# A prepared seam, table products by halves, twelve gathers, masks placed by ScalarE and an own order for the last routing chunk

## The reference, cut to what matters

```python
x = x + 0.5 * ffn(layernorm(x))
x = x + attention(layernorm(x))
x = x + 0.5 * ffn(layernorm(x))
```

```python
def ffn(xf):                                   # xf: 8192 x 256
    scores = softmax(xf @ gate_w.T)            # 64 experts
    _, idx = top_k(scores + gate_b, 6)
    # every expert takes its first 128 (token, choice) pairs, in the order of tokens
    h  = silu(xb @ w1[e].T) * (xb @ w3[e].T)   # 128 x 176, for each expert
    y[tok] += (h @ w2[e].T) * scores[tok, e]
    z  = silu(xf @ ws1.T) * (xf @ ws3.T) @ ws2.T   # shared expert, all tokens
    return y + z
```

## Time and profile before

| | |
|---|---|
| runs | 1922.69, 1925.52, 1930.68 us (median 1925.52) |
| profiled execution, its own time | 1931.83 us |
| its span | 1929.7 us |
| TensorE busy | 1792.8 us (93%) |
| VectorE, ScalarE, GpSimd busy | 1340.3, 1090.6, 837.2 us |
| mean granted TensorE clock | 0.973 |

### The profile page before, as it was taken

How to read it: one execution, slowest core, us unless ns; L and a number is a source line. 1 busy time by engine, 2 the same in 40 slices (tenths; PEclk the granted TensorE clock), 3 DMA queues, 4 the chain that set the end, 5 groups by cost and what they waited for, 6 DMA issues and landing times. The chain is left out here.

```text
span 1929.7 us, 31890 instructions
## 1 busy us (share of the span) xinstructions
PE 1792.8 (93%) x10553; PEld 1098.0 (57%) x10554; DVE 1340.3 (69%) x3338; ACT 1090.6 (57%) x2260; POOL 837.2 (43%) x923
## 2 busy tenths in 40 slices
PE   5999999999957889999999999999799999989998
PEld 3565665777643345555555555555356666667776
DVE  4887878566547567777777777767278787766665
ACT  4767766111113667777777777777467676731111
POOL 1010100678664666656556665550001010037777
PEclk9999999999988899999999999999899999999999
DMA  2423331899853333333333333332222343339997
GB/s 76 125 84 117 117 109 70 228 261 259 231 126 88 88 84 105 104 102 108 108 98 109 105 100 101 89 89 57 66 72 84 110 124 103 98 109 263 267 262 158
DMA packets 192653, 244.05 MB, mean 126 GB/s; under 512 B 17578, under 2 KB 159978, under 8 KB 192494
## 3 DMA queue, kind: packets, MB, share of 16 engines
q1 hardware_dynamic: 166654, 202.97, 35.0%
q0 software_dynamic: 24576, 37.77, 10.2%
q10 hardware_dynamic: 1264, 1.31, 0.2%
HBM read 126.63 MB, written 63.86 MB: 99 GB/s over the span
## 5 line engine op out<-in xcount | busy, mean ns | idle before, releaser
L1359 DVE TENSOR_REDUCE a_smax<-a_p_ring 128x1 f32<-128x512 f32 (+2 forms) x768 | 355.2, 506 | 131.8 <-PE a_p_ring L1446 126.4
L1263 ACT ACTIVATE a_probs<-a_p_ring 128x512 f32<-128x512 f32 x640 | 368.1, 608 | 108.6 <-PE a_p_ring L1458 107.3
L48 POOL TENSOR_TENSOR f_rstd<-f_mv,eps 128x4 f32<-128x4 f32 x32 | 26.9, 840 | 543.0 <-DVE f_mv L42 538.4
L1446 PE MATMUL a_p_ring<-p_ks,p_qs 100*128 100x512 bf16 (+3 forms) x1024 | 244.7, 304 | 16.7 <-DVE a_smax L1359 5.2
L1458 PE MATMUL a_p_ring<-p_qs,p_ks 103*128 103x512 bf16 (+3 forms) x1024 | 242.9, 304 | 7.9 <-ACT a_probs L1263 6.3
L648 ACT ACTIVATE e_silu<-e_p_up 128x176 f32<-128x176 f32 x128 | 40.6, 317 | 352.8 <-PE e_p_up L738 352.8
L487 PE MATMUL f_p_up<-f_xnT,ws1T 128*128 128x512 f32 x384 | 187.9, 612 | 1.1 <-ACT f_xnT L280 1.1
L528 PE MATMUL f_p_z<-ws2T,f_hidden 128*128 128x256 f32 (+1 forms) x768 | 184.8, 391 | 1.8 <-DVE f_hidden L374 1.8
L127 POOL DMA_INDIRECT h_got<-rows,slot_token x128 | 126.0, 985 | 133.6 <-DVE slot_token L464 86.1
L487 PE MATMUL f_p_up<-f_xnT,ws3T 128*128 128x512 f32 x384 | 181.5, 595 | 0.0
L738 PE MATMUL e_p_up<-h_w,e_xT 128*128 128x352 f32 x512 | 176.8, 469 | 2.6 <-DMA h_w<-w_in 2.6
(11 more groups left out here) (156 smaller groups left out, 3579.1 us busy)
## 6 DMA issues: line engine op xcount, KB each, us to landing
h_w<-w_in SPq DMA_DIRECT2D x128, 352.0 KB
p_qs<-a_parts SPq DMA_DIRECT2D x192, 128.0 KB, 2.4
p_ks<-a_parts SPq DMA_DIRECT2D x192, 128.0 KB, 2.4
h_w<-w_in SPq DMA_DIRECT2D x128, 176.0 KB
rows<-f_row SPq DMA_DIRECT2D x32, 640.0 KB, 6.4
x<-x_in SPq DMA_DIRECT2D x16, 512.0 KB, 5.6
acc<-x SPq DMA_DIRECT2D x16, 512.0 KB, 3.3
a_x<-acc SPq DMA_DIRECT2D x16, 512.0 KB, 3.9
```

The costliest lines, as they stand in the source:

```text
L1263: nc.scalar.activation(to[:], p_score[s][:], ACT.Exp, scale=SCALE).then_inc(score_free[s], 1)
L1359: ins = nc.vector.tensor_reduce(smax[:, t, 4 * g + h:4 * g + h + 1], p_score[s][:, at:at + length], AX.X, ALU.max)
L1446: ins = nc.tensor.matmul(p_score[s][:, at:at + length], qs[1 - u][0:SR + MASK, 4 * g + h, t * P:(t + 1) * P], ks[1 - u][0:SR + MASK, 4 * g ...
```

## The change

1. Halves: add_to_table(c, r) does half of a chunk's 24 products, and TensorE puts one half in front of each turn.
2. Prepared seam: in attention's last turn new steps HEAD_STATS (at 0.72 of the turn: VectorE's statistics and GpSimd's scales of f2's chunk 0, after a wait for its load) and HEAD_NORM 0 to 3 (at 0.83 to 0.92: ScalarE normalises a tile each). f2 skips these for chunk 0.
3. Twelve gathers (GATHERS) ahead instead of eight, with twelve buffers.
4. ScalarE masks: place_masks is gone; ScalarE copies the mask rows in 32 pieces of 7 partitions x 1024 elements, one behind each of experts 24 to 55 of e1.
5. Last chunk: in chunk 14 TensorE does up(15, 2), shared(14, 0), logits(15), shared(14, 1); chunk 15 has an order of its own. ScalarE does write_down(14) behind exponents(15), and silus(15, 1) last; VectorE's add_shared(14, 1) goes behind picked, multiply(15, 1) behind slots. hidden of j = 2 has two buffers.
6. VectorE: pick compares with an operand that is doubled in its innermost place; the ranks' sum is two additions and a shorter sum; the table is finished in three operations instead of four.
7. The semaphore redirected is gone (a drain on VectorE instead), and attention's x are arrivals.x[2:4].

```diff
@@ scalar, route_and_share @@
 def chunk(c, i, u, left):
     exponents(c)
+    if not left:
+        write_down(c - 1)
     silus(c, 0)
     if left:
         normalise(c + 1, *later(i, u, 1))
-    silus(c, 1)
     if left:
+        silus(c, 1)
         evacuate(c + 1, 0)
         evacuate(c + 1, 1)
     cap(c)
-    write_down(c)
+    if left != 1:
+        write_down(c)
     if left:
         logits(c + 1)
         silus(c + 1, 2)
+    else:
+        silus(c, 1)
@@ vector @@
-    if c:
+    if c and left:
         add_shared(c - 1, (c - 1) % XR, 1)
...
-    nc.vector.tensor_copy(topf[:], topi[:, :, 0:K])
+    nc.vector.tensor_copy(topf[:], topi[:, :, 0:K].unsqueeze(3).to_broadcast([P, NT, K, 2]))
...
+    by_twos = [P, NT * K, E // 2, 2]
+    nc.vector.tensor_tensor(pick[:].rearrange("p t k (e n) -> p (t k) e n", n=2),
...
+    if not left:
+        add_shared(c - 1, (c - 1) % XR, 1)
     multiply(c, 0)
-    multiply(c, 1)
+    if left:
+        multiply(c, 1)
...
+    nc.vector.tensor_tensor(half_sum[:], by_pair[:, :, 0:E // 2], by_pair[:, :, E // 2:E], ALU.add)
+    nc.vector.tensor_tensor(half_sum[:, :, 0:E // 4], half_sum[:, :, 0:E // 4],
+                            half_sum[:, :, E // 4:E // 2], ALU.add)
-        nc.vector.tensor_reduce(rank[:], prod[:], AX.X, ALU.add)
+        nc.vector.tensor_reduce(rank[:].rearrange("p t k -> p (t k)"), half_sum[:, :, 0:E // 4],
+                                AX.X, ALU.add)
@@ behind the last chunk @@
     slots(N - 1)
-    add_shared(N - 1, (N - 1) % XR, 0)
+    multiply(N - 1, 1)
     dve.wait_ge(table_added, N)
...
-    add_shared(N - 1, (N - 1) % XR, 1)
+    for r in range(2):
+        add_shared(N - 1, (N - 1) % XR, r)
@@ tensor @@
     up(c, 1)
-    if left:
-        turn(c + 1, 0)
-    if c:
-        add_to_table(c - 1)
-    if left:
-        turn(c + 1, 1)
+    for r in range(2):
+        if c:
+            add_to_table(c - 1, r)
+        turn(c + 1, r)
     ranks(c)
-    shared(c, 0)
-    if left:
+    if left > 1:
+        shared(c, 0)
         up(c + 1, 2)
     else:
-        add_to_table(c)
+        up(c + 1, 2)
+        shared(c, 0)
+        logits(c + 1)
     shared(c, 1)
+def last_chunk(c):
+    up(c, 0)
+    add_to_table(c - 1, 0)
+    add_to_table(c - 1, 1)
+    ranks(c)
+    up(c, 1)
+    add_to_table(c, 0)
+    add_to_table(c, 1)
+    shared(c, 0)
+    shared(c, 1)
@@ experts @@
-                    if pre and e == E - 2 * LANES:
-                        place_masks(sp, w, pre)
+                    if pre and 0 <= e - MASKS_FROM < MASK_PIECES:
+                        place_mask(nc, act, pre, e - MASKS_FROM)
@@ attention @@
+NEXT_STAGE = [(0.72, ("HEAD_STATS",)), (0.83, ("HEAD_NORM", 0)), (0.86, ("HEAD_NORM", 1)), (0.89, ("HEAD_NORM", 2)),
+              (0.92, ("HEAD_NORM", 3))]
-            (B - 1, place(OUTPUTS, TAIL + LATE_MAXIMA)),
+            (B - 1, place(OUTPUTS, TAIL + LATE_MAXIMA + NEXT_STAGE)),
+                        elif kind == "HEAD_NORM":
+                            if step[1] == 0:
+                                act.wait_ge(arrivals.head_scales_ready, 1)
+                            token_normalise(nc, arrivals.x[0], arrivals.head_rstd, arrivals.head_shift,
+                                            arrivals.first_row, [step[1]])
+                        elif kind == "HEAD_STATS":
+                            dve.wait_ge(arrivals.x_loaded[0], 16 * (B // XR) + 16)
```

More of the change, by code:

```diff
@@ L30 @@
 LANES = 8
+GATHERS = 12
 GROUP = 4
@@ L96, in open_handover @@
     to.x_loaded, to.x_rounds = arrivals.x_loaded, layer * B // XR
-    to.gathered, to.gather_rounds = arrivals.gathered, layer * E // LANES
+    to.gathered = arrivals.gathered
+    to.gathers_past = [layer * len(range(s, E, GATHERS)) for s in range(GATHERS)]
     to.weights_loaded, to.first_load = arrivals.weights_loaded, layer * E
@@ L156, in route_and_share @@
         x = to.x
-        row = [sb(f"row{u}", [P, NT, ROW]) for u in range(2)]
+        row = [to.first_row, sb("row1", [P, NT, ROW])]
         stats = sb("stats", [P, NT, 6])
@@ L184, in route_and_share @@
         silu = [sb(f"silu{n}", [P, T]) for n in range(RING)]
-        hidden = [sb(f"hidden{j}", [P, T]) for j in range(3)]
-        table = sb("table", [P, 2, E])
+        hidden = [[sb(f"hidden{j}", [P, T])] for j in range(2)] + [[sb(f"hidden2{n}", [P, T]) for n in range(2)]]
+        table = sb("table", [P, E])
         empty = sb("empty", [P, E])
@@ L272, in _ @@
                 pool.wait_ge(slot_token_ready, 1)
-                for e in range(LANES):
+                for e in range(GATHERS):
                     gather_rows(nc, w, dram, to, e)
@@ L390, in add_shared @@
                                                    ALU.add).then_inc(acc_ready, 1)
-                statistics(0, 0, 0)
+                if head_ready:
+                    dve.sem_inc(stats_ready, 1)
+                else:
+                    statistics(0, 0, 0)
                 set_up()
@@ L992, in load_attention, with place_mask @@
         sp.dma_start(to[:], fro).then_inc(pre.weights_loaded, 16)
[L995 to L1004 removed]
+MASK_HEADS = 2
+MASK_PIECES = 4 * H // MASK_HEADS
+def place_mask(nc, act, pre, piece):
+    if piece == 0:
+        act.wait_ge(pre.mask_ready, 1)
+    rows, heads = slice(SR, SR + MASK + TOP), piece % (H // MASK_HEADS) * MASK_HEADS
+    which = piece // (H // MASK_HEADS)
+    to = (pre.qs[0], pre.ks[0], pre.qs[1], pre.ks[1])[which]
+    ins = nc.scalar.copy(to[rows, heads:heads + MASK_HEADS, :],
+                         pre.mask16[rows, which % 2, :].unsqueeze(1).to_broadcast([MASK + TOP, MASK_HEADS, T]))
+    if piece == MASK_PIECES - 1:
+        ins.then_inc(pre.mask_placed, 1)
 def set_up_attention(nc, dve, w, pre, piece):
@@ L1041, in attention @@
         ident16, qs, ks, v, smax_parts = pre.ident16, pre.qs, pre.ks, pre.v, pre.smax_parts
-        x = [sb(f"x{n}", [P, NT, D]) for n in range(2)]
+        x = arrivals.x[2:4]
         residual = [sb(f"residual{n}", [P, NT, D]) for n in range(2)]
```

117 lines of the change are left out of this document (66 added, 51 removed).

## The result

| | before | after |
|---|---|---|
| median of the runs | 1925.52 us (1922.57 to 1930.68, 7 runs) | 1908.43 us (1902.63 to 1915.96, 7 runs) |
| ratio, 95% interval | | 0.9906, 0.9889 to 0.9923 |
| profiled execution, own time and span | 1931.83, 1929.7 us | 1908.43, 1906.6 us |
| TensorE busy | 1792.8 us (93%) | 1789.8 us (94%) |
| mean granted TensorE clock | 0.973 | 0.976 |

The forecast was 1913.0, range 1902 to 1922. The profiled execution of after is its median one, that of before stood 6.3 above its own. So the spans differ by 23.1 us, and the medians by 17.1.

What follows compares the result with a forecast made beforehand. TensorE, busy for 93% of the span, was taken as the bound. Terms summing to -12.4 took the profiled 1931.8 us to 1919.4, which stands 6.3 above the median, so 1913 us, range 1902 to 1922.

Steps and rivals of the forecast that it cites:

- the clock in the tails: Last chunk of f1 and f2: TensorE's clock falls while it is thinly busy, +1.2 us a stage, +2.4 in all.
- the seam: Attention to f2: ScalarE's prepared normalisation waits for chunk 0's load, delaying attention's tail and lowering the clock; +2.8 us.
- the twelve gathers: GpSimd before the experts: SyncE's last store hides the longer gathers, and later scatters cost nothing; 0 us.
- Halves: Routing chunks 1 to 14, two stages: half the table's products fill TensorE's wait, 0.42 us a chunk, -11.8 us.
- Pick: VectorE's comparison falls from 1.76 to 0.96 us, which shows only in chunk 0 of each routing stage; -1.6 us.
- The last chunk: Chunk 15: VectorE's addition delays the maximum, so experts start at 32.3 instead of 30.1 us; sum +3.1 us.
- Masks: Stage e1: ScalarE's mask copies remove TensorE's waits and half-speed products at no cost; -7.3 us, bounds -4 and -8.
- Rival A: Attention to f2: load and scales are ready when ScalarE comes; -9.7 instead of +2.8, 1900.5 us; chance 0.13.
- Rival B: Last chunk has no idle time, saving 1.9 us twice: -3.8 instead of +5.5, 1904 us; chance 0.12.
- C: Routing chunks: halves only move the wait to the second turn, none of the 11.8 us comes; 1925 us; chance 0.09.
- D: Stage e1: ScalarE's mask copy exceeds 2.35 us and lengthens 32 experts; at 3.5 us, 1950 us; chance 0.04.
- E: VectorE's comparison stays at 1.76 us; chunk 0 gains nothing, tails lose 0.8 each; 1916 us; chance 0.07.

Runs made afterwards that it cites:

- e11_no_halves: Changed kernel with eight gathers and the table's products undivided between the two turns; 1923.63 us, ratio 0.9971 to the kernel before.
- e12_old_pick: Changed kernel with eight gathers and pick's comparison again using an operand broadcast innermost; 1913.26 us, ratio 0.9939 to the kernel before.
- e4_new_tail: Changed kernel with VectorE's addition of shared(14, 0) behind the maximum and up(15, 0) before shared(14, 1); 1909.49 us, ratio 0.9898 to the kernel before.
- e5_before_again: The kernel before, unchanged, run again on chip 2 for its profile; 1929.24 us (one execution).
- e7_gathers8: Changed kernel with eight gathers ahead instead of twelve; 1910.59 us, ratio 0.9925 to the kernel before.
- e8_sp_masks: Changed kernel with masks placed by SyncE in four transfers of seven partitions; 1925.90 us, ratio 0.9994 to the kernel before.
- e10_best1: Changed kernel with eight gathers, earlier f2 loads, tiles in attention's tail, VectorE's addition behind the maximum, up(15, 0) earlier, own bank for shared(15, 1); 1894.60 us, ratio 0.9831.
- e2: Not a run here: the kernel's second experts stage, with the same 64 experts as the first; 204.26 us in the profile of the kernel before.
- e1_early_load: Changed kernel with the loads of f2's chunks 0 and 1 issued one attention turn earlier; 1919.14 us, ratio 0.9934 to the kernel before.
- e9: Changed kernel with eight gathers, f2's loads one turn earlier and its four first-row tiles in attention's tail; 1902.46 us, ratio 0.9880 to the kernel before.
- e6_after_again: The changed kernel, unedited, run again on chip 2; 1918.84 us, ratio 0.9953 to the kernel before.
- e3_old_tail: Changed kernel with chunks 14 and 15 in the kernel before's order on all three engines; 1914.24 us, ratio 0.9924 to the kernel before.

## Why the prediction was right or wrong

The number held: the terms add up to -12.4, against -17.1 in the first medians and -10.2 on chip 2. It held partly by luck. Two terms that failed, the clock in the tails and the seam, made the forecast some 7 us too slow. A third, the twelve gathers, made it some 8 us too fast where they cost anything. On chip 2 the errors cancel; on the first chip, where the gathers cost nothing, the time came out 4.6 us under the forecast. Term by term:

- **Halves, -11.8: right,** measured -10.8 (e11_no_halves). The two turns of a chunk stand 1.43 us apart (1657.88 and 1659.31), as drawn; the period fell by 0.385 instead of 0.42.
- **Pick, -1.6: right.** It takes 0.96 us, as chosen from prod. e12_old_pick gives 0.8 a tail, which is inside the next term, and 0.4 in chunk 0 of f2 and 0.8 in that of f1.
- **The last chunk, +3.1: right.** Each point of the layout was met within 0.5 us, the end within 0.1. In e4_new_tail, with the addition behind the maximum, the maximum comes at 7.1 instead of 9.8, so the addition's place is what held it. Additions and sum took 1.47 us (0.56, 0.36 and 0.55), where I had 1.4. The estimate of 1.2 in the prediction used only one row of its page. The Trainium skill, VectorE: DVE Perf Modes, on the trn2 errata, says right below that row that it comes out too low for a single operation and that the fixed part was measured as about 150 cycles, not 58; an estimate by that is 1.47 us, and the trace agrees.
- **The clock in the tails, +2.4: wrong.** The step "I take it that it falls here" failed: with waits of 1.39 and 0.91 us and products between, the clock stayed at 1.00 in both tails, and the term is 0. (The layout had TensorE busy for 1.54 of 4.3 us there, a little over the third that the text says; from 1674 to 1678 it was busy for 1.70 of 4.)
- **Masks, -7.3: the size right,** -7.3 in the first profile, once the 1.3 us that e1 gained in its first expert are taken out, -9.3 between e5_before_again and e7_gathers8, and -7.9 by the ratios of e8_sp_masks. The place was right in the first two. In e8_sp_masks the cost stands at the seam behind e1, as GpSimd's backlog, where the forecast had no term.
- **The seam from e1 to attention, no term:** the first profile gained 3.3 us there, and which change brings it is open. GpSimd's last scatter stands 5.4 to 5.7 us behind the last join before, 2.5 to 3.4 with ScalarE's masks and twelve gathers, but 3.0 to 5.7 with ScalarE's masks and eight (e10_best1 and e11_no_halves are the ends). So twelve gathers have a share, and ScalarE's masks alone need not bring it.
- **Twelve gathers, nothing: wrong.** I looked for their cover at the barrier and found it, and did not ask what stands behind them at the start of the experts. They cost 6.3 us in e1 and 3.1 in e2 on chip 2, less 1.3 at the seam to attention, and nothing on the first chip.
- **The seam, +2.8: wrong, about -2.** The first step held: ScalarE waited at HEAD_NORM 0 (3.81 us, 4.4 forecast), the last exponential ends 5.8 us later (6.5 forecast), and WO starts 6.5 us later, measured from the turn in front of the exponentials. What failed is that the tail "needs some 3.7 more": the clock was at 0.50 from 1356 to 1358, which made the products with the values 1.2 us longer, but at 1.00 again when WO ran. So it was in all eight profiles of the seam as drawn. In the one profile of e1_early_load it came back only at the end of WO, and WO and the products in front of it paid some 4 us.

Rival A was half right: the seam pays, and pays 6 us more where the tiles stand in the tail. Its -9.7 has a slip: by its own terms it is 4.4 for the turn and 3.3 for the clock, -7.7. Rival B's 1.9 us a stage against the kernel before were not reached by the order as drawn (1.8 longer from logits(14) to the experts), half of them by e4_new_tail (0.95 shorter) and all by e10_best1 (2.05 shorter). C, D and E are refuted, by e11_no_halves, by copies of 1.04 us, and by pick's 0.96.

What stays open: no kernel with eight gathers and nothing else changed ran on chip 3, so e9, e11 and e12 are held against e7_gathers8 by stages of the traces and not in the same runs.

## What to carry to other kernels

Lay out the lists of all engines at a change of order: a short operation placed in front of the one that others wait for (here an addition in front of a maximum) undid a reordering on another engine. Put work prepared for the next stage where its engine has a hole and nothing of this stage stands behind it, not merely where its input is ready. A deeper prefetch is not free because it is hidden at one barrier: read the first microseconds of the stage that follows, on more than one chip.

## What the runs showed of the hardware

- Behind a wait of 1.82 us TensorE's granted clock was at 0.50 in one tail (e1_early_load), and behind waits of 1.39 and 0.91 us with products between them it stayed at 1.00 in another. At the barrier to f2 it fell in nine of the eleven profiles with a prepared seam, and chunk 0 took 10.4 to 10.5 us from its first turn to its logits; in e4_new_tail and e8_sp_masks it stayed at 1.00 and they took 7.75 and 7.74. Nothing in the lists of these engines differs there.
- The same holds at f1's first chunk. Its first products of the second layer in the changed kernel, in the same kernel again and in e7_gathers8, whose lists are the same up to there (TensorE's timelines):

```profile
35.43 5.49 PE L574 MATMUL f_p_z<-ws2T,f_hidden 128*128 128x256 f32 x12 [0.46 <-DVE f_hidden L406]
```
```profile
35.74 3.95 PE L574 MATMUL f_p_z<-ws2T,f_hidden 128*128 128x256 f32 x12 [0.26 <-DVE f_hidden L406]
```
```profile
35.45 2.87 PE L574 MATMUL f_p_z<-ws2T,f_hidden 128*128 128x256 f32 x12 [0.61 <-DVE f_hidden L406]
```

  The clock was at 0.50 for some 7 us, for 3 us and not at all, and from logits(0) to logits(1) it is 23.4, 21.6 and 20.5 us. So single profiles of the same work differ by up to 2.9 us here and 2.7 at the barrier to f2, with the clock as the only difference that the rows show, and a gain of 2 us can't be read from one pair.
- With twelve gathers on GpSimd's queue, ScalarE and VectorE began the first experts up to 5 us after their inputs were complete, and the rows name no engine of the core for it. That the gathers bring it is shown on one chip by e7_gathers8; by what way they do is open, and why the first profile has none of it too. Two ways that no run here tells apart are the gathers' own transfers and the transfers of the queues that the profile lists as "instruction" (1.41 and 0.61 MB in e6_after_again).
- GpSimd's queue goes through eight gathers in at most 4.1 us and through twelve in 5.95 (e3_old_tail), long before the gathers themselves are done (they start 1.25 us apart in the timeline).
